# Score steps of two attention stages joined on PE, and two local stages cut in two parts each

## The reference, cut to what matters

```python
y = x.reshape(b, t, nh, hs).transpose(0, 2, 1, 3)
scores = jnp.einsum('bhtk,bhsk->bhts', y, y) / math.sqrt(hs)
attn = jax.nn.softmax(scores, axis=-1)
o = jnp.einsum('bhts,bsc->bhtc', attn, x)          # self; o @ weight
...
scores = jnp.einsum('bhqd,bhkd->bhqk', Q, K) * scale
scores = jnp.where(mask[None, None], scores, jnp.float32(-jnp.inf))   # cross
...
x = x + o @ wo                                     # local layer, twice
h = shift_token(x)
h = (h - mu) / jnp.sqrt(var + 1e-05) * lg + lb
a, g = jnp.split(h @ w1 + b1, 2, axis=-1)
x = x + (a * jax.nn.gelu(g, approximate=False)) @ w2 + b2
...
x = _layernorm(x + _L0_attn_ref(x, L0_attn_weight), axis=-1)
x = _layernorm(x + _L0_xattn_ref(x, ctx_1024, ctx_1024, ...), axis=-1)
x = _layernorm(x + _L0_ffn_ref(x, ...), axis=-1)
```

## Time and profile before

| | |
|---|---|
| median of 3 runs | 1535.69 us (1531.51 to 1535.7) |
| the profiled execution | 1535.67 us |
| its span, first to last instruction | 1533.9 us |
| PE busy | 1377.0 us (90%), 11993 matmul records |
| PEld busy | 938.6 us (61%) |
| DVE, ACT, POOL busy | 1004.8 (66%), 952.5 (62%), 880.1 us (57%) |
| mean granted TensorE clock | 0.959 of 2.4 GHz |

### The profile page before, as it was taken

How to read it: one execution, slowest core, us unless ns; L and a number is a source line. 1 busy time by engine, 2 the same in 40 slices (tenths; PEclk the granted TensorE clock), 3 DMA queues, 4 the chain that set the end, 5 groups by cost and what they waited for, 6 DMA issues and landing times. The chain is left out here.

```text
span 1533.9 us, 38526 instructions
## 1 busy us (share of the span) xinstructions
PE 1377.0 (90%) x11993; PEld 938.6 (61%) x12088; DVE 1004.8 (66%) x2900; ACT 952.5 (62%) x2562; POOL 880.1 (57%) x1289
## 2 busy tenths in 40 slices
PE   4778999999999999999999999999999999998764
PEld 2445666666666666666666666666666666666553
DVE  1446677676677776766776767767767677677432
ACT  1234666676666766766667667666676676666642
POOL 1034556666665567666655676666555766665533
PEclk8678999999999999999999999999999999999975
DMA  4000000000000000000000000000000000000000
GB/s 146 11 5 4 5 7 5 5 2 5 5 5 5 5 3 5 2 5 5 5 5 5 3 5 2 5 5 5 5 5 3 5 2 5 5 4 4 3 3 4
DMA packets 21645, 12.47 MB, mean 8 GB/s; under 512 B 5816, under 2 KB 20834, under 8 KB 21474
## 3 DMA queue, kind: packets, MB, share of 16 engines
q1 hardware_dynamic: 21600, 11.95, 2.6%
HBM read 9.84 MB, written 2.10 MB: 8 GB/s over the span
## 5 line engine op out<-in xcount | busy, mean ns | idle before, releaser
L787 ACT ACTIVATE local_e<-local_ps,local_bias,local_rn 128x128 f32<-128x128 f32 x512 | 229.0, 491 | 18.1 <-DVE local_bias L961 18.0
L1109 POOL TENSOR_TENSOR local_rn<-local_sc,half_neg 128x8 f32<-128x8 f32 x128 | 212.7, 1662 | 7.5
L1127 POOL TENSOR_TENSOR local_e<-local_e,local_rd 128x512 f32<-128x512 f32 x128 | 133.0, 1040 | 134.5 <-DVE local_rd L965 133.3
L956 DVE TENSOR_REDUCE local_m<-local_ps 128x4 f32<-128x512 f32 x128 | 88.6, 692 | 104.6 <-PE local_ps L648 104.6
L569 PE MATMUL self_ps<-self_z,self_e 128*128 128x129 f32 x1024 | 147.5, 288 | 1.7 <-DVE self_y L890 0.8
L890 DVE SCALAR_TENSOR_TENSOR self_y<-self_ps,self_rd,self_y 128x128 f32<-128x128 f32 x448 | 133.2, 345 | 9.2
L569 PEld LDWEIGHTS self_ps<-self_z,self_e 128*128 128x128 f32 x1024 | 129.0, 197 | 15.8 <-issue 7.8
L1026 POOL TENSOR_SCALAR local_x<-local_out 128x256 f32<-128x256 f32 x32 | 12.9, 404 | 216.3 <-issue 216.3
L942 DVE TENSOR_TENSOR local_cosp<-local_ps,cos_t 128x512 f32<-128x512 f32 x128 | 87.2, 682 | 71.7 <-ACT local_sq L770 71.7
L556 PE MATMUL self_ps<-wz,self_kT 128*128 128x512 f32 x256 | 128.4, 626 | 1.8 <-ACT self_kT L732 1.8
L787 ACT ACTIVATION_READ_ACCUMULATOR local_e<-local_ps,local_bias,local_rn 128x1 f32 x512 | 122.4, 239 | 0.0
(11 more groups left out here) (173 smaller groups left out, 3436.1 us busy)
## 6 DMA issues: line engine op xcount, KB each, us to landing
self_xin<-x SPq DMA_DIRECT2D x32, 64.0 KB, 1.7
cross_cin<-ctx_in SPq DMA_DIRECT2D x32, 64.0 KB, 1.8
out<-local_out SPq DMA_DIRECT2D x32, 64.0 KB, 1.6
wqkv_s<-wqkv SPq DMA_DIRECT2D x2, 768.0 KB
wz<-w_heads SPq DMA_DIRECT2D x1, 1024.0 KB, 5.6
w_r<-w SPq DMA_DIRECT2D x2, 341.0 KB
con<-consts SPq DMA_DIRECT2D x1, 644.0 KB, 3.6
wo_s<-wo SPq DMA_DIRECT2D x2, 256.0 KB
```

Of the source, the lines that this page charges most:

```text
L787: nc.scalar.activation(s.e[:, a, p, :], bank[:, 128 * p:128 * p + 128], ACT.Exp, bias=s.bias[:, a, p:p + 1], scale=s.rq[:, a, p:p + 1], ac ...
L956: nc.vector.tensor_reduce(s.m[:, a, :], bank.rearrange("p (c t) -> p c t", c=LH // 2), AX.X, ALU.max, negate=True)\
L1109: nc.gpsimd.tensor_tensor(s.rn[:, heads], s.sc[:, heads], half_neg[:, 0:LH], ALU.pow).then_inc(done, 8)
L1127: nc.gpsimd.tensor_tensor(s.e[:, a, :, :], s.e[:, a, :, :], s.rd[:, a, :].unsqueeze(2).to_broadcast([128, LH // 2, 128]), ALU.mult)\
```

## The change

The cross and self score steps leave their stages on PE and become a part of their own, `joint_scores` (letter J). It emits the first pair of groups of S and C together, sixteen matmuls that alternate over four row groups and write four banks, and so on for the four blocks; the masks and the transposes of the maxima stand in steps of their own, so that the order can put other work between them. On the other engines the steps of S and C stay as they were and only their order changes.

Local attention is cut behind the transposes of k (head A, B; tail D, E) and the MLP behind the transpose of `local_hn` (head M, N; tail O, P). The table `SKEW` says how many iterations behind its part stands: M now works on sample i-3, in the iteration of A and D, and its tail O on i-4 in the next. No arithmetic is added or removed.

```diff
+LETTERS = ("ADMO", "BENP")
+SKEW = {"S": 1, "C": 2, "A": 3, "D": 3, "M": 3, "O": 4, "B": 4, "E": 4, "N": 5, "P": 5}
...
-    "MANAANMNMANMNMCSCBSSBCCSSBCCSABCACSCAASBBCSCBBSCSSCSASBCASSBABAB")
+    "NAOOANAPOPSABSPBCSBCSSAAJJDDBJJBJJBEJJEDJDJDSSCCSSDSESECMEEM")
...
-                    for g in pair:
+                    for s, g in groups:
                         rows = slice(32 * g, 32 * g + 32)
                         last = nc.tensor.matmul(scores_bank(s, g)[:, 128 * j:128 * j + 128], s.qmb[rows, j, :], s.kb[rows, :],
                                                 start=(j == 0 and not s.windowed), stop=(j == GH - 1), skip_group_check=True)
...
+            def joint_scores(v, w):
+
+                both = [s for s, u in ((SELF, v), (CROSS, w)) if u is not None]
+                pairs = [[(s, g) for s in both for g in s.pairs[n]] for n in range(2)]
+                if w is not None:
+                    pe.wait_ge(CROSS.k_ready, w + STEP)
+                    pe.wait_ge(CROSS.low, w + STEP)
+                    pe.wait_ge(CROSS.q_wide, w + STEP)
+                    mask_band(CROSS.even)
+                    mask_band(CROSS.odd)
+                yield
+                if v is not None:
+                    pe.wait_ge(SELF.z_ready, v + STEP)
+                    pe.wait_ge(SELF.k_ready, v + STEP)
+                    pe.wait_ge(SELF.low, v + STEP)
+                    pe.wait_ge(SELF.q_wide, v + STEP)
+                head_scores(pairs[0])
+                yield
+                if w is not None:
+                    pe.wait_ge(CROSS.max_done, w + 8)
+                    mask_band(CROSS.even)
+                    mask_band(CROSS.odd)
+                yield
+                if v is not None:
+                    pe.wait_ge(SELF.max_done, v + 8)
+                head_scores(pairs[1])
+                yield
+                if v is not None:
+                    pe.wait_ge(SELF.max_done, v + STEP)
+                    nc.tensor.transpose(SELF.even.bitcast(BF16)[:, 0:128], SELF.neg[:, :], ident_b[:, :])\
+                        .then_inc(SELF.neg_psum, STEP)
+                yield
...
+                if w is not None:
+                    pe.wait_ge(CROSS.neg_ready, w + STEP)
+                    mask_band(CROSS.even)
+                yield
+                if v is not None:
+                    pe.wait_ge(SELF.neg_ready, v + STEP)
+                turned_scores(pairs[0])
+                yield
...
+                if v is not None:
+                    pe.wait_ge(SELF.exp_done, v + 8)
+                turned_scores(pairs[1])
                 yield
```

More of the change, by code:

```diff
@@ L405, in decoder_kernel, with stages @@
         N_PREP_P = 5
-        def stages(eng, order, prepare_local, self_stage, cross_stage, local_attention, local_mlp):
+        def stages(eng, order, prepare_local, self_stage, cross_stage, attention_head, attention_tail, mlp_head, mlp_tail, joint_scores=None):
             def iteration(i):
                 parts = {}
[L411 to L414, removed]
+                if at(i, SKEW["S"]) is not None:
+                    parts["S"] = self_stage(at(i, SKEW["S"]))
+                if at(i, SKEW["C"]) is not None:
+                    parts["C"] = cross_stage(at(i, SKEW["C"]))
+                if joint_scores is not None and (at(i, SKEW["S"]) is not None or at(i, SKEW["C"]) is not None):
+                    parts["J"] = joint_scores(at(i, SKEW["S"]), at(i, SKEW["C"]))
                 for l in range(2):
[L416 to L419, removed]
+                    for letter, part in zip(LETTERS[l], (attention_head, attention_tail, mlp_head, mlp_tail)):
+                        v = at(i, SKEW[letter])
+                        if v is not None:
+                            parts[letter] = part(l, v)
                 weave(order, parts)
@@ L487, in head_scores, with turned_scores @@
                             last.then_inc(s.scores_n_psum, 4)
-            def turned_scores(s, pair):
-                for g in pair:
+            def turned_scores(groups):
+                for s, g in groups:
                     rows = slice(32 * g, 32 * g + 32)
@@ new lines, in joint_scores @@
+                yield
+                if v is not None:
[4 more added lines that the diff above has]
+                if w is not None:
+                    pe.wait_ge(CROSS.max_done, w + STEP)
+                    nc.tensor.transpose(CROSS.even.bitcast(BF16)[:, 0:128], CROSS.neg[:, :], ident_b[:, :])\
+                        .then_inc(CROSS.neg_psum, STEP)
+                    mask_band(CROSS.odd)
```

86 lines of the change are left out of this document (37 added, 49 removed).

## The result

The changed kernel takes 1541.85 us (median of 6 runs, 1540.09 to 1544.7); the kernel before, on the same chip, 1533.58 (6 runs, 1530.75 to 1535.7). The ratio is 1.0064, 95% interval 1.0051 to 1.0077: slower. The forecast was 1507, its range ended at 1537.

A forecast was written before the change was run, and what follows sets the result against it. TensorE's work plus its waits bounds the 43.72 us period; -3.0 - 2.35 + 2.3 + 0.8 + 0.7, 0.2 less for small stops, gives 42.0, clock +0.7 gives 42.7; over 28 iterations 28.6 us off 1535.7, so 1507, range 1477 to 1537.

The forecast's parts named there:

- the other nine iterations: Iterations outside the 28 that hold every stage: counted as no change, within 6 us either way.
- the clock: PE around the first joint fp32 block: falls to 1.2 GHz, 1.0 us in two iterations of three, +0.7 us a period.
- Joining: Joint score blocks on PE: fp32 -1.9, bf16 -0.9, fewer switches -0.2, together -3.0 us an iteration.
- Rival 3: Joint fp32 blocks: four-group products run as two pairs, 2.8 us more an iteration, 1566 us; chance 0.10.
- The rule that spoke against it: Joint bf16 blocks: matmul starts never closer than about 25 ns, so sixteen take 0.40 us and gain 0.2, not 0.9.
- New wait ahead of T0: PE before the first joint fp32 block: waits 2.3 us for DVE's maxima of both stages, mostly at L536, L541.
- rival 4: One more unseen wait of 1 us, behind GpSimd or ACT, leaves nothing measurable: 1535 us; chance 0.08.
- no wait at L541: Transposes of the maxima on PE: no wait there would mean DVE's chain was misread and the gain is larger.
- (a): Local 1's projection on PE (L689): waits for ACT's copy of the weighted values, +0.8 us an iteration.
- (b): Shift of M at the iteration's end: waits for DVE's last weighted sum of self, +0.7 us an iteration.
- The MLP term: MLP stretch on PE: 3.2 us lost, including eight exposed block tails of 0.17; all but 0.85 recovered, -2.35 us.
- Rival 1: Clock holds at 2.4 GHz throughout: period 42.0 us, 1488 us; chance 0.24.

The follow-up runs named there:

- experiment 4: Changed kernel with each joint block emitted as self's pair, then cross's: 1643.34 us; the same with eight idle matmuls ahead of local 1's query transposes: 1569.26 us.
- experiment 1: Changed kernel with GpSimd (POOL) rotating local 1's queries ahead of its second root: 1556.96 us, ratio 1.0169 to the kernel before.
- experiment 5: Changed kernel with idle matmuls in three waits: nine ahead of local 1's query transposes, three before the `local_oT` wait, three behind cross's output product: 1492.24 us.
- experiment 2: Changed kernel with nine idle matmuls on PE ahead of local 1's query transposes: 1502.58 us, ratio 0.9798 to the kernel before.
- experiment 6: Changed kernel with local 1's v product moved behind the second joint bf16 block and ACT's copy behind the first exponentials, no work added: 1515.93 us.
- experiment 7: Changed kernel with DVE, ACT and PE reordered around the joint blocks, GpSimd rotating local 1's queries earlier, three idle matmuls in each of three places: 1662.58 us.

## Why the prediction was wrong, by its own steps

The forecast was 42.7 us a period and nothing for the other nine iterations; measured were 44.39 us and, outside the 27 periods, -12.6 us. 1.69 us x 28 = 47, and 1507 + 47 - 12.6 = 1541. The 1.69 has two halves: 0.83 in the period without the clock (42.83 for 42.0) and 0.86 in the clock (1.56 for 0.7). Either alone would have left the time inside the range.

- **Joining, -3.0 us off PE: right, as far as the blocks show it.** In an iteration without a fall PE is busy 38.23 us against 10.20 + 31.14 = 41.34 of before, -3.1 in all. Both fp32 blocks cost 0.96, and running the pairs in turn costs 0.96 each (experiment 4). Rival 3 is out. The bf16 blocks cost what I took, but what that was worth alone no run here shows.
- **The rule that spoke against it: the trace disagrees.** Sixteen bf16 matmuls start in four rounds of four, the first at 718.13 and the last at 718.31, 0.06 us apart, so 15 ns a matmul; "TensorE: Matmul & The Clock Gate" of the Trainium skill, section "Wait — 56ns, not 53.3ns?", has 25 ns as the least. The estimate of 1.12 us for four fp32 products, worked out from the Trainium skill's section "Measured speedup vs the span model" of the same page, was 0.16 too long.
- **New wait ahead of T0, +2.3 us: right in size, incomplete in cause.** It is 2.04 + 0.22 us. It appears at L649, behind POOL, which I had only as rival 4's unseen wait; experiment 1 shows that without it DVE's maxima hold PE as long. My sign "no wait at L541" came, but not the larger gain that I tied to it. J0 to T0 takes 3.64 + 4.45 = 8.1 us where I had 7.7: +0.4. Three engines deliver together there, and I had followed one.
- **Waits (a) and (b), +0.8 and +0.7: right.** The projection of local 1 waits 0.76 us for ACT's copy, the shift of M 0.68 for self's last sum (14.4/19, 13.0/19). At the shift for N 0.4 where I had 0.5.
- **Period without the clock, 42.0: measured 42.83. One of the two steps that failed, the tails.** The MLP term counted 8 x 0.17 = 1.36 us of exposed tails as lost and took most of it back. With the joining's 3.0 PE's busy time should then have fallen by 4.4; it fell by 3.1. The stops were mostly exchanged for others: an iteration of before has nine gaps over 0.1 us on PE, one of the changed kernel seven. As an estimate, two tails fewer are 0.3 us and not 1.36. The idle time made up for some of it: 42.84 - 38.23 = 4.6 us, where the sum has 2.3 + 0.8 + 0.7 + 0.85 and 0.34 left in attention, 5.0.
- **The clock, +0.7 us: the other step that failed.** Place and mechanism were right (1.24 of 3.40 us busy, then 3.40 at 0.50). Its size was not. I took 1.0 us in two iterations of three. It falls in 23 of the 27, one fall costs 44.18 - 42.83 = 1.35, and in six of them a second fall comes at the waits (a) and (b), which I had costed as waits only; four of the six take 46.5. Mean 44.39 - 42.83 = +1.56. My bound of 1.7 per fall held, my choice below it did not: the lost time does not lie inside the wait, because the fall starts about as the wait ends (in the iteration shown at 724.30, L649 at 724.21), over work that T0 stands behind. L649's four transposes take 0.88 us to the next block there, 0.49 in experiment 5. That this is the cause, not a companion, experiments 2 and 5 show: idle work in the waits gives back 39 and 50 us.
- **The other nine iterations, nothing within 6: wrong, by -12.6 us**, in my favour. That the split shortens filling and draining is argued only; no experiment isolates it. The traces show 23.7 us less at half clock there (127.5 to 103.8), of which at most half is lost time. Without these 12.6 us the change would have been 18 us slower.
- **Rival 1 (clock holds, 1488)** is the state that experiment 5 built, at 1492, but the closeness is luck: its period is 42.82 and not 42.0, and the 18.9 us from outside the periods, which I had at nothing, make up for it.
- **Two sums of the rivals are wrong as they stand.** Taking wait (a) and half the wait before T0 out of rival 1 is 0.8 + 1.15 = 1.95 us, 55 us in 28 iterations, so 1433 and not 1475. And rival 3 decides when T0 and T1 together cost 1.7 us more, which is 2.0 each rather than 0.96 + 0.22, not 1.8.

## What to carry to other kernels

Before taking a wait into the sum as its own length, ask how busy the engine is around it, and add what the work behind the wait costs at 1.2 GHz: here 1.35 us on top of a wait of 2.3, in 23 of 27 iterations, more than the change's whole net gain of 0.9 without falls. Work that is taken off TensorE while another engine's chain stays as long becomes a wait, so look first for independent matmuls to put there (experiment 6), and where none are left, idle ones are cheaper than the fall (experiment 5). When two chains are joined, list every engine that must deliver before the joint step; here three ended within 1.1 us, and neither try at speeding one up (experiments 1 and 7) gained anything, since each slowed another. A stop that moves to another place still exposes a tail: count the stops of the new order too before crediting those that go.

## What the runs showed of the hardware

- bf16 matmuls on different row groups do not keep program order: with eight of self ahead of eight of cross in the program, cross starts 0.03 us behind self, and the starts of both are interleaved up to the last (700.20 and 700.23). Of the fp32 pairs emitted in turn, cross's begins only 0.98 us behind self's (705.45), as self's ends; yet six of self's eight bf16 matmuls, which stand ahead of it in the program, start behind it (705.49). Why fp32 pairs take turns and bf16 ones do not no run here shows.
- Four row groups at once cost nothing over two: 0.96 us for four fp32 blocks of 512 columns, the same as for two.
- Ahead of T0 three idle matmuls (0.6 us), with POOL's order of experiment 1, left the clock at 2.4 GHz in 25 of 27 iterations; experiment 1 without them has it there in two.
